# A fused four-stage kernel: the router worked in between the attention's steps, FP4 rounding shared with GpSimd, group 0's prediction ahead of the output product, the norm's affine part on ScalarE, the rates' bias as a product with a row of ones

## What is computed

```
x = x + local_attention(norm(x))   # 16 heads, each row attends to itself and its two neighbours
x = x + experts(norm(x))           # router: softmax over 8 experts, the 2 best; hidden width 1024, exact gelu
x = x + delta_attention(norm(x))   # own layernorm with ln_w, ln_b; see below
x = x + fp4_feed_forward(norm(x))  # gate, up (256 -> 704), silu, down; input, hidden and weights rounded to FP4

# delta_attention, per head of 64 and time step, with two states S and R:
alpha, aR   = sigmoid(xn @ Wa.T + ba), sigmoid(xn @ WaR.T + baR)     # the decay rates
pred = S kn;  r = clip(v - pred, -1, 1)
S = alpha * S;  S = S + beta  * kn (v - kn S)
R = aR * R;     R = R + gamma * kn (r - kn R)
o = S q + R q;  out = o @ Wo.T

# FP4: blocks of 16, scale = max|x|/6, nearest of 0, .5, 1, 1.5, 2, 3, 4, 6, times scale
```

## Time and profile before

| | us |
|---|---|
| median of 3 runs | 4022.38 (4015.97 to 4025.67) |
| profiled execution, its own time | 4007.19 |
| its span in the trace | 4005.4 |
| PE busy | 3264.1 (81%) |
| DVE busy | 2633.9 (66%) |
| ACT busy | 1427.6 (36%) |
| POOL busy | 891.3 (22%) |
| mean granted clock of PE | 0.929 of full speed |

### The profile page before, as it was taken

One profiled execution on the slowest core, in us unless ns is written; L12 is line 12 of the kernel. 1 busy time (PEld: TensorE's weight loads), 2 busy tenths in 40 slices (PEclk: granted clock), 3 DMA queues, 4 the chain that ended last, 5 costly groups with the idle time before them and its releaser, 6 DMA issues. The chain is left out here.

```text
span 4005.4 us, 141798 instructions
## 1 busy us (share of the span) xinstructions
PE 3264.1 (81%) x62854; PEld 2462.9 (61%) x62854; DVE 2633.9 (66%) x5780; ACT 1427.6 (36%) x3252; POOL 891.3 (22%) x1018
## 2 busy tenths in 40 slices
PE   7844999993888888888888888888888888727777
PEld 4633999992566666666655666666566566514555
DVE  6844000002877887887787778877877787667887
ACT  1111212221444454445444444544454444311111
POOL 2316222221223222222322232222223222200000
PEclk9965999996899999999999999999999999858999
DMA  2154666652000000000000000000000000010000
GB/s 63 48 184 143 185 182 179 182 160 89 5 7 11 7 7 11 7 7 7 11 7 7 7 11 7 7 11 7 7 7 11 7 7 5 6 40 14 22 21 14
DMA packets 101423, 172.44 MB, mean 43 GB/s; under 512 B 15128, under 2 KB 75160, under 8 KB 100752
## 3 DMA queue, kind: packets, MB, share of 16 engines
q1 hardware_dynamic: 72592, 127.75, 9.8%
q0 software_dynamic: 19824, 23.03, 4.0%
q10 hardware_dynamic: 8400, 12.58, 0.9%
HBM read 125.35 MB, written 40.05 MB: 41 GB/s over the span
## 5 line engine op out<-in xcount | busy, mean ns | idle before, releaser
L962 POOL TENSOR_TENSOR da_M<-da_M,da_decay 128x512 f32<-128x512 f32 x256 | 279.9, 1122 | 634.8 <-DVE da_M L1125 323.1
L1268 ACT COPY da_Ub<-da_U 32x256 f32<-32x256 f32 x1024 | 412.0, 402 | 17.4
L1102 DVE TENSOR_TENSOR da_eGn<-da_eGn,da_z 128x30 f32<-128x30 f32 (+14 forms) x960 | 352.6, 367 | 33.0
L643 DVE TENSOR_SCALAR moe_y<-moe_ps_dn,moe_zs 128x256 f32<-128x256 f32 x71 | 34.4, 484 | 510.1 <-PE moe_ps_dn L769 510.1
L1101 DVE TENSOR_TENSOR da_z<-da_eGn 128x30 f32<-128x30 f32 (+14 forms) x960 | 348.7, 363 | 27.6
L1554 PE MATMUL da_C<-da_Ub,da_Km 128*64 128x256 f32 x2048 | 302.8, 417 | 23.3 <-ACT da_Ub L1268 9.5
L759 PEld LDWEIGHTS moe_ps_up<-moe_zsT,moe_up 128*128 128x128 f32 x2272 | 266.2, 193 | 5.4 <-ACT moe_zsT L676 1.8
L759 PE MATMUL moe_ps_up<-moe_zsT,moe_up 128*128 128x128 f32 x2272 | 266.9, 276 | 1.2 <-ACT moe_zsT L676 1.2
L1386 PE MATMUL da_unit<-da_wx,da_xnT 128*128 128x512 f32 x512 | 257.8, 628 | 3.7 <-DVE da_sp L1045 2.7
L769 PE MATMUL moe_ps_dn<-moe_down,moe_hT 128*128 x1136 | 256.8, 379 | 0.0
L1393 PE MATMUL da_unit<-da_xnT,da_wx 128*128 128x128 f32 x2048 | 245.5, 279 | 12.4 <-ACT da_eGn L1253 12.4
(11 more groups left out here) (289 smaller groups left out, 6830.4 us busy)
## 6 DMA issues: line engine op xcount, KB each, us to landing
moe_up<-in_upT SPq DMA_DIRECT2D x71, 1024.0 KB, 5.1
moe_zs<-moe_slots SPq DMA_DIRECT2D x71, 129.0 KB, 4.2
moe_down<-in_downT ACTq DMA_DIRECT2D x8, 1024.0 KB, 12.0
la_x<-in_x SPq DMA_DIRECT2D x16, 256.0 KB, 3.9
stream<-la_y SPq DMA_DIRECT2D x32, 128.0 KB, 2.3
moe_x<-stream SPq DMA_DIRECT2D x8, 512.0 KB, 4.9
da_x<-moe_acc SPq DMA_DIRECT2D x128, 32.0 KB, 2.0
stream<-da_xz SPq DMA_DIRECT2D x128, 32.0 KB, 1.8
```

Source lines behind the costliest of these rows:

```text
L962: ins = nc.gpsimd.tensor_tensor(st_, st_, decay[:, par, rec, 2 * g:2 * g + 2].rearrange("p a b -> p (a b)").unsqueeze(2).to_broadcast([P, ...
L1102: c.link(tt(Xm[:, s + 1:C, 0:s], Xm[:, s + 1:C, 0:s], t, ALU.add))
L1268: ins = nc.scalar.copy(Ub[rows_of(b), :, :, b, :], U[rows_of(b), rec])
```

## The change

**Stages one and two are joined.** One block (names `le_`) does both. The router of group g, whose four tiles are the pairs 2g and 2g+1, is spread over the attention's steps: `moments2(g)` and `roots2(g)` in step 2g+3, `router_rows`, `turned_rows` and `logits` in 2g+4 with `shift`, `exps2` in 2g+5, `choose` in 2g+6, `ranks` and `place` in 2g+7, `scatter(g)` in 2g+8. The router's normalised rows are written by ACT for both copies, not by DVE and copied by ACT. The result of the attention stays in SBUF for the router and is stored once, straight to `acc`. The pads go as plain DMAs on ACT's queue, with their addresses loaded into a register, and not as indirect DMAs on POOL. Some buffers become single, and the experts' down weights are loaded once the attention's slots are free.

The diff, cut to the calls that set the order:

```diff
         @block.gpsimd
         def _(pool):
+            for s in STEPS:
+                if part_of(s, 8) is not None:
+                    scatter(part_of(s, 8))
+                if here(s - 1):
+                    residual(s - 1)
+                if here(s + 3):
+                    roots(s + 3)
+                if part_of(s, 3) is not None:
+                    roots2(part_of(s, 3))
...
-            for e in range(E):
-                nc.gpsimd.indirect_dma_start(slots[:], bass.IndirectOffsetOnAxis(ap=padidx[:, e:e + 1], axis=0), pad[:], None).then_inc(padded, 16)
...
         @block.scalar
+            for s in STEPS:
+                if part_of(s, 4) is not None:
+                    router_rows(part_of(s, 4), 0)
+                if here(s - 2):
+                    turned_out(s - 2)
+                if part_of(s, 5) is not None:
+                    exps2(part_of(s, 5))
+                if here(s - 1):
+                    exps(s - 1)
+                if part_of(s, 4) is not None:
+                    turned_rows(part_of(s, 4), 0)
+                if here(s + 3):
+                    normalised(s + 3)
+                if part_of(s, 4) is not None:
+                    turned_rows(part_of(s, 4), 1)
+                if here(s + 2):
+                    turned(s + 2)
+                if part_of(s, 4) is not None:
+                    router_rows(part_of(s, 4), 1)
...
+            for e in range(E):
+                at = act.value_load(padidx[0:1, e:e + 1], min_val=0, max_val=DUMP)
+                act.dma_start(slots[bass.ds(at, P), :], pad[:]).then_inc(padded, 16)
```

```diff
-                c.link(nc.vector.tensor_scalar(xn[:], z[:], mv[:, 1, 0:1], rstd[:, 1:2], ALU.subtract, ALU.mult))
-                c.link(tt(xn[:], xn[:], lnw[:], ALU.mult))
-                tt(xn[:], xn[:], lnb[:], ALU.add).then_inc(xn_ready, 1)
-
-            def add_bias(n, u):
-                need(dve, a_psum, n * 4 + u + 1)
-                cols = slice((u % 2) * 512, (u % 2 + 1) * 512)
-                tt(sp[:, u // 2, cols], un[:, RATE_BANK[u]], ba[:, u // 2, cols], ALU.add).then_inc(a_ready, 1)
+                nc.vector.tensor_scalar(xn[:], z[:], mv[:, 1, 0:1], rstd[:, 1:2], ALU.subtract, ALU.mult).then_inc(xn_ready, 1)
...
             def copy_xT(n, par):
                 need(act, xT_psum, n + 1)
-                nc.scalar.copy(xnT[:, par], un[:, 1, 0:D].rearrange("p (k t) -> p k t", k=KD)).then_inc(xT_ready, 1)
+                for kk in range(KD):
+                    ins = nc.scalar.activation(xnT[:, par, kk, :], un[:, 1, kk * P:(kk + 1) * P], ACT.Identity, bias=lnb[:, kk:kk + 1], scale=lnw[:, kk:kk + 1])
+                ins.then_inc(xT_ready, 1)
...
+                mm(bank, ones[:], ba[:, u // 2, cols], start=True, stop=False)
                 for kk in range(KD):
-                    ins = mm(bank, xnT[:, par, kk, :], wx[:, kk, u // 2, cols], start=(kk == 0), stop=(kk == KD - 1))
+                    ins = mm(bank, xnT[:, par, kk, :], wx[:, kk, u // 2, cols], start=False, stop=(kk == KD - 1))
                 ins.then_inc(a_psum, 1)
```

```diff
+                pool.wait_ge(z_scaled, t + 1)
+                pc.link(nc.gpsimd.tensor_tensor(zlevel[:], zratio[:], zmagic[:], ALU.add))
+                pc.link(nc.gpsimd.tensor_tensor(zlevel[:], zlevel[:], zmagic[:], ALU.subtract))
+                if t > 0:
+                    pool.wait_ge(zT_psum, t * 2)
+                nc.gpsimd.tensor_tensor(blocks(qz[:].rearrange("p u d -> p (u d)")), blocks(zlevel[:]),
+                                        zscl[:].unsqueeze(2).to_broadcast([P, WIDE // FP4_BLOCK, FP4_BLOCK]), ALU.mult).then_inc(qz_ready, 1)
...
-                if u == 1 and t + 1 < TRIPS:
+                if u == 0 and t + 1 < TRIPS:
                     norm(t + 1)
                 round_h(n)
-                if u == 2 and t + 1 < TRIPS:
+                if u == 1 and t + 1 < TRIPS:
                     round_z(t + 1)
```

More of the change, by code:

```diff
@@ L188, in _ @@
                 if here(s + 3):
                     roots(s + 3)
-                if here(s - 1):
-                    residual(s - 1)
+                if part_of(s, 3) is not None:
+                    roots2(part_of(s, 3))
+            for i in range(4):
+                pool.wait_ge(stored[i], 32 * (NPAIR // 4))
+            pool.wait_ge(cleared, 32)
+            for n in range(SLOT_TILES):
+                b = n % 2
+                pool.wait_ge(ye_ready, n + 1)
+                if n > 0:
+                    pool.wait_ge(added[1 - b], 16 * ((n - 1) // 2 + 1))
+                nc.gpsimd.indirect_dma_start(acc[:], bass.IndirectOffsetOnAxis(ap=zs[:, n % ZB, D:D + 1].bitcast(U32), axis=0),
+                                             ye[:, b, :], None, compute_op=ALU.add).then_inc(added[b], 16)
@@ L193, in _ @@
+            for b in range(2):
+                pool.wait_ge(added[b], 16 * ((SLOT_TILES - b + 1) // 2))
         @block.vector
@@ L281, in _ @@
+            for n in range(SLOT_TILES):
+                dve.wait_ge(zs_loaded[n % ZB], 16 * (n // ZB + 1))
+                weigh(n)
         @block.scalar
@@ L731, in _ @@
+                if part_of(s, 4) is not None:
+                    logits(part_of(s, 4))
+            need(pe, idx_ready, GROUPS)
+            mm(ps_cnt, ones[:], before[:, (GROUPS - 1) % 2, ST, :], start=True, stop=True).then_inc(count_psum, 1)
             pe.wait_ge(table_ready, 1)
             for i in range(3):
-                ins = nc.tensor.matmul(ps_h[0:1, i * P:(i + 1) * P], table[:, i:i + 1], ident[:], start=True, stop=True)
+                ins = mm(ps_tab[:, i * P:(i + 1) * P], table[:, i:i + 1], ident[:], start=True, stop=True)
@@ L996, in period @@
                     rescale(i, par, 3)
+                if put:
+                    put_out(i - 1)
                 if prepare:
@@ L1205, in _ @@
             norm_last(0)
-            for u in range(4):
-                add_bias(0, u)
             every_period(period)
@@ L1319, in period @@
                     solved(i, 1, 0)
+                if put:
+                    result(i - 1)
+                if state:
                     solved(i, 1, 1)
@@ L1634, in period @@
                     state_update(i, 1, 0)
+                if put:
+                    result(i - 1)
+                if state:
+                    solve(i, 1, 1)
+                    inner_outputs(i, par, 1, 0)
                 if prepare:
@@ L1700, in _ @@
             pe.wait_ge(loaded, 16 * LOADS)
+            pe.wait_ge(cleared, 1)
             turn_x(0)
```

749 lines of the change are left out of this document (349 added, 400 removed).

## The result

The changed kernel takes 4045.43 us (median of 10 runs, 4032.3 to 4063.43) against 4017.23 for the kernel before, timed beside it (10 runs, 4010.31 to 4025.67). The ratio is 1.0067, interval 1.0047 to 1.0086: **28 us slower**, where 63 us faster was forecast. Its profiled execution took 4048.02 us, span 4046.2, mean granted clock 0.921. TensorE is busy 3446.8 us (85%), 183 more than before; DVE 2483.7 (61%), 150 less; ACT 1467.3; POOL 945.2.

What follows compares the result with a forecast made beforehand. Bounds taken: POOL's scatters in the router, TensorE's work plus short handshakes in delta, DVE busiest in the feed forward. Terms -47 + 16 - 3 - 29 = -63 against 4007.2 gave 3944, expected median about 3960 us; range 3895 to 4015.

Steps and rivals of the forecast that it cites:

- rivals 3 and 4: Delta stage: 3, move hidden, bias half paid, 4021 us, chance 0.08; 4, bias wholly paid, 4061 us, chance 0.07.
- part 2: Delta stage: bias products +3.8 us per period, less 2.9 and 0.4 gained, +0.5 per period, +16 us in all.
- The closed handshakes: Delta stage: earlier `inner_predicted` lets DVE get ahead, taking 2.9 of TensorE's 3.96 us of waits per period away.
- the load's -3: Start of the delta stage: smaller loads give -3 us.
- the 0.4 for the output product at full clock: Delta stage: the moved output product no longer falls half to 1.2 GHz, 0.4 us less per period.
- Rival 4: Delta stage: bias products wholly on TensorE's path, no wait closes, +3.8 us per period, +118, total 4061; chance 0.07.
- upper bound: Router between the attention steps: the -41 us end of its bounds, -54 to -41, around the forecast -47.
- stretched scatters: Router: scatters beside a working DVE cost 1.5 to 2.0 us instead of 1.26, giving back up to 13; half taken.
- the order on POOL: Router, even steps 8, 10, 12: `normalised` waits for POOL's chain with eight scatters, 10.1 us; each step +8.25.
- lower bound: Feed forward: if three or four DVE operations are stretched beside POOL, a trip gives only 2.7 us, 19 in all.
- The 2.8 left for `round_z` on DVE: Feed forward: 6.2 us of `round_z` stand where DVE has 2.6 spare; with 0.8 of lag, 2.8 per trip left.
- The 1.2 for the clock: Feed forward: the down product behind the gap takes 5.31 us instead of 3.05; half taken, about 1.2 per trip.

Runs made afterwards that it cites:

- e5: The kernel before with only the rates' bias as a float32 product over one row, DVE's four additions gone: 4131.35 us, ratio 1.0288.
- e11: e5 without the product: ACT reads the rates from PSUM, DVE adds nothing, the bias is left out of the result: 3957.20 us, ratio 0.9879.
- e14: e5 with the product over 128 equal bias rows and a weight of 1/128 in place of one row: 4087.30 us, ratio 1.0178.
- e10: The changed kernel with the bias as one bf16 product over 96 rows, three holding the bias's bf16 parts: 3888.10 us, ratio 0.9695 to before.
- e2: The kernel before with the whole delta stage change alone (bias product, affine part on ScalarE, moved output product): 4092.23 us, ratio 1.0182.
- e1: The kernel before with the joined attention and router alone: 3979.04 us, ratio 0.9896.
- e13: e8 with each group's scatters behind `residual` and `roots` on POOL instead of ahead of them: 3934.94 us, ratio 0.9795 to before.
- e8: The changed kernel with the rates' bias added by DVE again as before: 3934.68 us, ratio 0.9811 to before.
- e3: The kernel before with the feed forward change alone: 4002.63 us, ratio 0.9951.

## Why the prediction was wrong

The forecast was -63, measured are +27. Of the 90 between, 60 lie in the delta stage, 9 in the feed forward and 5 in the router; the other 16 lie between the sum of the three parts and the whole, within their intervals. The result falls between rivals 3 and 4. Each figure below that comes from timed runs is good to about 10 us.

**The step that failed** is in part 2: "one added product is two passes, about 0.96, and four 3.8 us per period". The price was bounded only from below ("could be cheaper, down to nothing"). It is dearer: 164 us by e5 less e11, where 3.8 x 31 gives 118. That is +46 of the error. The row from which it was taken, L1386, is one over 128 rows; for such rows it is near (3.85 in e14's period). The rule of the Trainium skill, "TensorE: Matmul & The Clock Gate", section "Why this matters for your kernels", that 32 rows take as long as 128, pointed the right way: few rows are no cheaper. It speaks of 32 rows; here, with one float32 row, the edit cost 116 us against 72 over 128 rows, so the rows do matter, and the measurement decides.

**The closed handshakes** I put at 2.9 + 0.4 = 3.3 per period, all from the move, with the load's -3 105 us. e10 is -123; less -42 for the router and -20 for the feed forward, its delta part is -61, and without the bf16 product's 0.22 x 128 = 28 it is -89, or 2.9 per period (-76, if one counts that the rates products behind it are quicker too, 592 ns on average against 618 in the earlier trace rows). So the sum was near, +16 of error or somewhat more, but its source was not: "it buys nothing by itself", said of DVE's additions, is refuted by e11 (-49), while the moved product and the affine part gave -24, with a new wait for `da_KmT` and TensorE at 1.2 GHz behind it. Of the 0.4 for the output product at full clock little came: 406 ns on average in after, 415 in the earlier trace rows, 0.14 for its 16 instructions, and 4.20 us in the period shown, where I had 3.7. I had asked what closes when the product leaves its place, and not what TensorE then reaches too early.

**Delta in sum.** +13 forecast against e2's +73. Of the 60, 46 and 16 are the two terms above, to within the noise. Rival 4 had the products wholly on the path and 2.9 per period as the point from which it decides; the period grew by 2.97. Its total, 4061, was too high, since the handshakes that it left open did close.

**Router.** Forecast -47, e1 -42, 1 us from the upper bound. That is partly luck. The steps were longer than I laid out: the last result came at 308.6, forecast 289.7, the last scatter ended at 345.3, forecast 327.0, the first expert matmul started at 360.55, forecast 335.3. Of the 25 us by which I missed it, 7 had been taken off already for stretched scatters, and 14 lie in the two executions compared, that of before 12 under its median and that of after 2 above its own. Of the causes I took, stretched scatters fell (median 0.96 as before), and the order on POOL is worth little (e13). Steps that I had put at 14.75 took 13.8 to 17.0, and four and not three took 20.4 to 21.7. In these four ACT's copy of the turned outputs (L547) starts 3.4 to 4.8 us after TensorE's products have ended, with nothing in the trace that releases it in between. But in e8's profile, of the same block, it follows them within 0.15 us in these steps, and steps 8 to 14 together are as long (130.2 us, 130.7 in after): the lag only moved time from one step to its neighbour. What makes the steps longer than laid out stays open.

**Feed forward.** Forecast -29, e3 -20, in the direction of its lower bound. A trip gained 2.6 us (48.9 to 46.2), where I took 4.4. Three terms were mis-sized. The 2.8 left for `round_z` on DVE: the wait behind it was 3.83. The 1.2 for the clock did not come, as the down product behind it took 5.75 and 4.71 in turn. And the wait for TensorE's copies, which was to vanish, went from 6.1 to 8.7 us; the one for the rounded hidden row (L1953), which I had left out, from 5.6 to 12.6. Stretched DVE operations came as foreseen, two of them by 1.7 and 1.6 us; POOL's took 2.34 to 2.46, inside the 1.7 to 2.9 of the forecast. (The Trainium skill, "GPSIMD Engine Reference", section "Key points", has POOL contend with VectorE's instructions that have two SBUF inputs or run in a 2-port mode. L1790, which was held, has two inputs; L1792, held too, has one, and no run here shows its mode.)

## What to carry to other kernels

In a stage that TensorE bounds, work added to TensorE is paid at least one for one, and a bias that looks free because it takes one row was the dearest edit here; if it must be a product, one bf16 pass over the value's three parts takes 0.22 us where the float32 one took 1.05. Price a moved piece of work from both sides: the wait that it fills, and the product that its engine now reaches too early. Time the parts of a joint change apart, since two gains of 42 and 20 us hid behind one loss of 73.

## What the runs showed of the hardware

- A float32 product over one row with 512 columns costs more than one over 128 rows: 1.05 us against 0.96, and 1.98 against 1.88 for the product behind it, whose weight load starts only with its matmul (after and e14). Over 128 products it was 44 us by the timed runs, 31 between the profiled executions.
- One bf16 pass of 512 columns over 96 rows costs 0.22 us in the same place (e10).
- POOL operations of 128x1024 float32 (2.34 to 2.46 us) stretch two of DVE's of 128x704, 0.89 to 2.63 with two inputs and 0.53 to 2.14 with one; a reduction of that size, 0.89, is not stretched. POOL's indirect DMAs keep their median of 0.96 us while DVE works.
- Single executions of the same router code differ by up to 18 us in the stages up to its end, as the first expert load shows (383.65, 400.15, 401.56).
